# Layer normalisation in two rounds of four tiles instead of four rounds of two, and half of a preload moved to another queue

## The chip, the cores and the metric

The kernel runs on the 8 cores of one Trainium2 chip. Each core works on its own 1024 of the 8192 tokens, with all weights; the cores exchange nothing. The metric is the device time in microseconds (us) of the slowest core. A core has TensorE (PE, matmuls), VectorE (DVE), ScalarE (ACT), GpSimd (POOL) and SyncE (SP). SP, ACT and POOL issue transfers (DMA), each from a queue of its own; the profile names them q1 (SP), q10 (ACT) and q0 (POOL).

## The reference

```python
xn = _layernorm(x)                                   # over 4096 features
s  = einsum('bsk,nk->bsn', xn, weight * block_mask)  # 4096 x 4096, mask of 32x32 blocks
gt = einsum('th,ih->ti', xn, w_gate) * s_gate        # 11008 x 4096
u  = einsum('th,ih->ti', xn, w_up) * s_up
h  = silu(gt) * u
f  = einsum('ti,hi->th', h, w_down) * s_down         # 4096 x 11008
out = x + s * silu(f)
```

x is 4 x 2048 x 4096 in float32; the three big weights are int32 with values up to 127.

## The kernel before

The program has four blocks with a barrier after each: "prep", "attn", "ffnA", "down".

**prep** (from line 121) makes xnT, the normalised x of the core, transposed and in bf16. The 1024 tokens are 8 tiles j of 128 tokens by 4096 features. There are four buffers xs (float32) and four xn (bf16), used as xs[j % 4] and xn[j % 4]; tiles 0 to 3 are loaded at the start, in pairs from SP (0, 2) and ACT (1, 3), and SP then loads the small constants. For a tile:
- VectorE sums it (L172) after its load. ScalarE squares it with an accumulated sum (L196); the squared values themselves go to xn[j % 4] as scratch, so for j of 4 and more this waits until tile j-4 is normalised and transposed.
- `stats` (L148 to L168) makes mean, variance, reciprocal root and shift from these sums in small instructions on VectorE, with the root on ScalarE (L201) between.
- ScalarE normalises it into xn (L207). TensorE transposes it in 32 pieces (L239), into four PSUM tiles p_tr of eight pieces each, and VectorE copies each p_tr to xnT (`evac_tr`, L147). TensorE writes p_tr[b] for the next tile only after the copy of p_tr[b] of the last.

Before the change `stats` runs on two columns (tiles 2b and 2b+1), for b from 0 to 3. VectorE's order is: sum 2b, sum 2b+1, stats b, then the copies of tiles 2b-2 and 2b-1. ScalarE's order (`half`) is two squares, root, two normalisations. Tiles 4 and 6 are loaded by SP as soon as tiles 0 and 2 are normalised. Tiles 5 and 7 are loaded by ACT, between the halves, after tiles 1 and 3 are normalised (L217). VectorE begins with three copies of transposed scale vectors (L136), which come from constants that SP loads behind its two tiles of x.

The semaphore p1s counts ScalarE's instructions; `s_sq`, `s_sqrt_b` and `s_xn` give the count at which a square, a root or a normalisation is done.

**attn** (from line 306) loads the mask and the weight, multiplies them, and makes s. **ffnA** (from line 470) makes h for 86 tiles of 128 inner features and stores each to hTd in DRAM.

**down** (from line 581) multiplies h with w_down, in 8 groups g of 512 output features. The first 48 tiles of h are loaded once into hTr, by six transfers r of 2 MB (eight tiles each, L587). The other 38 come anew for each g, in pairs through four buffers hTl (L605). SP issues the six transfers of hTr first and then the pairs; after pair 2 it issues four tiles of x (L615). TensorE takes the tiles in the order P4SEQ, which mixes resident and streamed ones: 0, 48, 1, 49, 2, ... so the first pair hTl is wanted for the second of 86 steps of a group. ScalarE has nothing to do in down before the first group of matmuls is complete.

Of the kernel before, what the change touches and what calls it, by code (L numbers as in the profile page):

```python
# [13 lines left out]
AX = mybir.AxisListType  # L14
# [22 lines left out]
def build_nc():  # L37
# [20 lines left out]
    with ExitStack() as top:  # L58
# [25 lines left out]
        with ExitStack() as s123:  # L84
# [3 lines left out]
            if True:  # L88
                with ExitStack() as s01:
# [23 lines left out]

                    t_vtr = lambda k: k + 1
                    t_trb = lambda j, b: 3 + 4 * j + b + 1
                    s_sq = lambda j: 5 * (j // 2) + (j % 2) + 1
                    s_sqrt_b = lambda b: 5 * b + 3
                    s_xn = lambda j: 5 * (j // 2) + 4 + (j % 2)
                    V = {}

                    with nc.Block("prep") as blk:
                        @blk.vector
                        def _(ve):
                            vc = 0
                            def inc(ins):
                                nonlocal vc
                                ins.then_inc(p1v, 1)
                                vc += 1
                                return vc
                            inc(ve.memset(eps_col[:, :], EPS))  # L130
                            inc(ve.memset(invd_col[:, :], 1.0 / D))
                            inc(ve.memset(ninvd_col[:, :], -1.0 / D))
                            for k, dst in enumerate([(sg_cols, NIT), (su_cols, NIT),
                                                     (sd_cols, 32)]):
                                ve.wait_ge(p1t, t_vtr(k))
                                V[f"vecev{k}"] = inc(ve.tensor_copy(  # L136
                                    dst[0][:, 0:dst[1]], p_vec[k % 2][:, 0:dst[1]]))
                            def evac_tr(jj):
                                for b in range(4):
                                    ve.wait_ge(p1t, t_trb(jj, b))  # L140
                                    dst = xnT[:, :].rearrange(
                                        "p (kc t) -> p kc t", t=T)[
                                        :, b * 8:(b + 1) * 8,
                                        jj * 128:(jj + 1) * 128]
                                    src = p_tr[b][:, :].rearrange(
                                        "p (c t) -> p c t", t=128)
                                    V[f"trev{jj}_{b}"] = inc(ve.tensor_copy(dst, src))  # L147
                            def stats(b, sl, sqrt_lm):  # L148
                                n_mean = inc(ve.tensor_scalar(
                                    st_mean[:, sl], st_sum[:, sl],  # L150
                                    ninvd_col[:, 0:1], None, ALU.mult))
                                inc(ve.tensor_scalar(st_msq[:, sl], st_ssq[:, sl],
                                                     invd_col[:, 0:1], None, ALU.mult))
                                ve.wait_ge(p1v, n_mean)
                                n_m2 = inc(ve.tensor_tensor(
                                    st_m2[:, sl], st_mean[:, sl],
                                    st_mean[:, sl], ALU.mult))
                                ve.wait_ge(p1v, n_m2)
                                V[f"var_{b}"] = inc(ve.tensor_tensor(
                                    st_var[:, sl], st_msq[:, sl], st_m2[:, sl],  # L160
                                    ALU.subtract))
                                ve.wait_ge(p1s, sqrt_lm)
                                n_rst = inc(ve.reciprocal(st_rst[:, sl],
                                                          st_sqv[:, sl]))
                                ve.wait_ge(p1v, n_rst)
                                V[f"nmr_{b}"] = inc(ve.tensor_tensor(
                                    st_nmr[:, sl], st_mean[:, sl], st_rst[:, sl],
                                    ALU.mult))  # L168
                            for b in range(4):
                                for j in (2 * b, 2 * b + 1):  # L170
                                    ve.wait_ge(sm_x[j % 4], 16 * (j // 4 + 1))
                                    V[f"sum{j}"] = inc(ve.reduce_sum(  # L172
                                        st_sum[:, j:j + 1], xs[j % 4][:, :], AX.X))
                                ve.wait_ge(p1s, s_sq(2 * b + 1))
                                ve.wait_ge(p1v, V[f"sum{2 * b + 1}"])
                                stats(b, slice(2 * b, 2 * b + 2), s_sqrt_b(b))
                                if b >= 1:
                                    evac_tr(2 * b - 2)
                                    evac_tr(2 * b - 1)
                            evac_tr(6)  # L180
                            evac_tr(7)

                        @blk.scalar
                        def _(sc):
                            for i in (1, 3):
                                sc.dma_start(xs[i % 4][:, :],
                                             d_x[i * 128:(i + 1) * 128, :]
                                             ).then_inc(sm_x[i % 4], 16)

                            def half(js, var_lm, nmr_lm):  # L190
                                for j in js:
                                    sc.wait_ge(sm_x[j % 4], 16 * (j // 4 + 1))
                                    if j >= 4:
                                        sc.wait_ge(p1s, s_xn(j - 4))
                                        sc.wait_ge(p1t, t_trb(j - 4, 3))
                                    sc.activation(xn[j % 4][:, :], xs[j % 4][:, :],  # L196
                                                  AF.Square,
                                                  accum_out=st_ssq[:, j:j + 1]
                                                  ).then_inc(p1s, 1)
                                sc.wait_ge(p1v, V[var_lm])  # L200
                                sc.activation(st_sqv[:, js[0]:js[-1] + 1],  # L201
                                              st_var[:, js[0]:js[-1] + 1], AF.Sqrt,
                                              bias=eps_col[:, 0:1]).then_inc(p1s, 1)
                                sc.wait_ge(p1v, V[nmr_lm])
                                for j in js:
                                    sc.wait_ge(p1s, s_sq(j))
                                    sc.activation(xn[j % 4][:, :], xs[j % 4][:, :],  # L207
                                                  AF.Identity,
                                                  bias=st_nmr[:, j:j + 1],
                                                  scale=st_rst[:, j:j + 1]  # L210
                                                  ).then_inc(p1s, 1)
                            for b in range(4):
                                half([2 * b, 2 * b + 1], f"var_{b}", f"nmr_{b}")
                                if b <= 1:
                                    i = 2 * b + 5
                                    sc.wait_ge(p1s, s_xn(i - 4))
                                    sc.dma_start(xs[i % 4][:, :],  # L217
                                                 d_x[i * 128:(i + 1) * 128, :]
                                                 ).then_inc(sm_x[i % 4], 16)

                        @blk.tensor
                        def _(te):
# [326 lines left out]
        with ExitStack() as s4:  # L549
# [31 lines left out]
            with nc.Block("down") as blk:  # L581
                @blk.sync
                def _(sy):
                    for r in range(6):
                        sy.wait_ge(sm_hT_st[0], 16 * (4 * r + 4))
                        sy.wait_ge(sm_hT_st[1], 16 * (4 * r + 4))
                        sy.dma_start(  # L587
                            hTr[:, r * 8192:(r + 1) * 8192].rearrange(
                                "q (i t) -> q i t", i=8),
                            d_hTd[8 * r:8 * r + 8, :, :].rearrange(  # L590
                                "i q t -> q i t")).then_inc(sm_hr[r], 16)
# [88 lines left out]

                @blk.scalar
                def _(sc):
                    for g in range(8):
                        sc.wait_ge(p4t, g * NIT + NIT)
                        for ht in range(4):
# [80 lines left out]
```

## Time and profile before

| | |
|---|---|
| median of 8 runs | 4368.04 us (4361.84 to 4985.66) |
| profiled execution | 4363.12 us |
| its span, slowest core (0) | 4361.3 us; the eight cores 4347.6 to 4361.3 |
| mean granted TensorE clock, core 0 | 0.973 |
| TensorE matmuls busy | 4054.6 us, 93% |
| VectorE busy | 694.2 us, 16% |
| ScalarE busy | 210.9 us, 5% |
| moved by the DMA engines | 599.17 MB |

The profile is one execution, on its slowest core. Busy time is that of compute instructions; the issue of a transfer is shown on a queue (SPq, ACTq). The time from issue to landing is not busy time of any engine. The time of the whole execution lies 1.8 us above the span of the slowest core.

### The profile page before, as it was taken

The numbers are of one execution on the slowest core, as the hardware profiler recorded it, in microseconds if no ns is written. First come the engines' busy times: TensorE is split into PE (matmuls) and PEld (weight loads), VectorE is DVE, ScalarE is ACT, GpSimd is POOL, SyncE is SP. The second block draws the span as 40 slices with busy tenths as digits, with TensorE's granted clock in tenths as the row PEclk, the third lists the DMA queues.
The fourth block names the chain that finished last, engine by engine and source line by source line (L and its number), as shares of the span: only waits on it lengthen the run. The fifth ranks groups of instructions, "written<-read, shape, count | busy, mean of one in ns | idle before, by whom it ended". The sixth has DMA issues, their size and how long they took to land.

```text
span 4361.3 us, 43080 instructions; the slowest of 8 cores (4347.6 to 4361.3 us)
## 1 busy us (share of the span) xinstructions
PE 4054.6 (93%) x18669; PEld 1847.5 (42%) x19043; DVE 694.2 (16%) x584; ACT 210.9 (5%) x267; POOL 239.1 (5%) x384
## 2 busy tenths in 40 slices
PE   2199998999999999999999999999599999999998
PEld 1044443444444444444444444444244444444443
DVE  5577530000000000000000000000000000000000
ACT  5000000000000000000000000000000000000000
POOL 0000000000000000000000000000011111111110
PEclk8599999999999999999999999999799999999999
DMA  4899634444444444444444444443778888887886
GB/s 156 292 339 326 224 135 87 87 87 87 86 84 84 84 84 85 85 86 86 87 87 87 87 87 87 87 87 78 207 156 184 194 176 164 191 197 153 185 195 133
DMA packets 205543, 599.17 MB, mean 137 GB/s; under 512 B 13156, under 2 KB 101552, under 8 KB 174000
## 3 DMA queue, kind: packets, MB, share of 16 engines
q0 software_dynamic: 120256, 287.33, 37.9%
q1 hardware_dynamic: 62928, 252.96, 17.3%
q10 hardware_dynamic: 22176, 56.11, 3.6%
q8 instruction: 155, 2.54, 0.2%
q14 instruction: 28, 0.23, 0.0%
HBM read 810.79 MB, written 47.71 MB: 197 GB/s over the span
## 4 chain that ended last, share of the span: by engine, by line
PE 80%; DMA 2%; DVE 1%; SPq 1%; issue 1%; ACT 0%; DVEq 0%; POOL 0%; ACTq 0%
PE p_g L503 27%; PE p_u L503 27%; PE p_acc L677 26%; DMA hTl<-hTd 2%; SPq L587 1%; DVE tmpm L711 0%; DVE outs L714 0%; ACT gTs L689 0%; DMA wub<-hwu 0%; DMA hTd<-hTt 0%; DVE uss L538 0%; ACT L689 0%; DVE hTt L546 0%; SPq L615 0%; POOL wgb L476 0%
## 5 line engine op out<-in xcount | busy, mean ns | idle before, releaser
L503 PE MATMUL p_g<-xnT,wgb 128*128 128x512 bf16 x5394 | 1198.3, 380 | 25.1 <-DMA wub<-hwu 19.3
L503 PE MATMUL p_u<-xnT,wub 128*128 128x512 bf16 x5394 | 1195.7, 379 | 5.8
L503 PEld LDWEIGHTS p_g<-xnT,wgb 128*128 128x128 bf16 x5504 | 540.0, 98 | 670.1 <-issue 23.3
L503 PEld LDWEIGHTS p_u<-xnT,wub 128*128 128x128 bf16 x5504 | 537.7, 98 | 650.2
L677 PE MATMUL p_acc<-hTr,wdb 128*128 128x512 bf16 x3010 | 719.4, 380 | 38.5 <-ACT gTs L689 18.3
L677 PE MATMUL p_acc<-hTl,wdb 128*128 128x512 bf16 x2384 | 576.4, 382 | 41.8 <-DMA hTl<-hTd 39.1
L677 PEld LDWEIGHTS p_acc<-hTr,wdb 128*128 128x128 bf16 x3072 | 301.0, 98 | 410.0 <-issue 55.6
L538 DVE TENSOR_SCALAR uss<-p_u,su_cols 128x512 f32<-128x512 f32 x172 | 121.2, 746 | 2162.6 <-PE p_u L503 2162.6
L370 PE MATMUL p_sT<-xnT,wtm 128*128 128x512 bf16 x2004 | 444.8, 381 | 9.6 <-DVE wtm L421 6.7
L677 PEld LDWEIGHTS p_acc<-hTl,wdb 128*128 128x128 bf16 x2432 | 239.0, 98 | 331.4 <-issue 49.5
L370 PEld LDWEIGHTS p_sT<-xnT,wtm 128*128 128x128 bf16 x2048 | 199.0, 98 | 244.8 <-issue 10.0
L711 DVE TENSOR_TENSOR tmpm<-gTs,sTl 128x1024 f32<-128x1024 f32 x32 | 39.2, 1225 | 1208.9 <-ACT gTs L689 1206.4
L522 ACT ACTIVATE sil<-p_g,sg_cols 128x512 f32<-128x512 f32 x172 | 108.9, 684 | 2239.4 <-PE p_u L503 2239.4
L476 POOL DMA_DIRECT2D wgb<-hwg x86 | 45.8, 532 | 2916.4 <-PE p_u L503 2247.6
L637 POOL DMA_DIRECT2D wdb<-hwd x174 | 128.9, 741 | 1166.7 <-PE p_acc L677 1059.0
L421 DVE TENSOR_TENSOR wtm<-wts,p_me 128x4096 bf16<-128x4096 f32 x32 | 141.5, 4421 | 74.4 <-PE p_sT L370 57.3
L394 DVE TENSOR_REDUCE red<-mk 128x128 f32<-128x4096 int32 x32 | 141.3, 4414 | 49.8 <-DMA mk<-mask 49.7
L546 DVE TENSOR_TENSOR hTt<-sil,uss 128x1024 bf16<-128x1024 f32 x86 | 105.4, 1225 | 10.4 <-ACT sil L522 1.6
L339 PE MATMUL p_bm<-red,gm_sb 128*4 128x128 f32 x64 | 14.5, 315 | 86.9 <-DVE bmfeT L408 55.5
L689 ACT ACTIVATE gTs<-p_acc,sd_cols 128x512 f32<-128x512 f32 x64 | 37.9, 703 | 1041.2 <-PE p_acc L677 1041.2
L239 PE MATMUL p_tr<-idb_sb,xn 128*128 128x128 bf16 x256 | 22.0, 267 | 50.1 <-DVE xnT L147 33.5
L479 POOL DMA_DIRECT2D wub<-hwu x86 | 46.3, 538 | 2.8 <-issue 2.8
(43 smaller groups left out, 280.0 us busy)
## 6 DMA issues: line engine op xcount, KB each, us to landing
wgb<-hwg POOLq DMA_DIRECT2D x86, 1024.0 KB, 9.2
wub<-hwu POOLq DMA_DIRECT2D x86, 1024.0 KB, 13.9
wdb<-hwd POOLq DMA_DIRECT2D x168, 512.0 KB, 7.5
hTl<-hTd SPq DMA_DIRECT2D x152, 512.0 KB, 6.1
mk<-mask SPq DMA_DIRECT2D x32, 2048.0 KB, 12.9
wts<-hwt SPq DMA_DIRECT2D x32, 2048.0 KB, 11.2
hTd<-hTt ACTq DMA_DIRECT2D x86, 256.0 KB, 10.3
xTl<-xT SPq DMA_DIRECT2D x32, 512.0 KB, 11.6
```

What stands on the lines that cost most here:

```text
L370: ins = te.matmul(p_sT[par][th][:, :], A, xnT[:, kb * T + th * 512: kb * T + th * 512 + 512], start=(kb == 0), stop=(kb == 31))
L394: ve.tensor_reduce(red[k % 2][:, :], mk[k % 2][:, :].rearrange("p (s e) -> p s e", e=32), AX.X, ALU.add).then_inc(p2v, 1)
L421: ve.tensor_tensor(wtm[par][:, :].rearrange("p (a b c) -> p a b c", a=32, b=4), wts[par][:, :].rearrange("p (a b c) -> p a b c", a=32, b=4 ...
L476: gp.dma_start(wgb[it % 2][:, :].rearrange("p (b i) -> p b i", i=128), d_hwg[it]).then_inc(sm_wg[it % 2], 16)
L479: gp.dma_start(wub[it % 2][:, :].rearrange("p (b i) -> p b i", i=128), d_hwu[it]).then_inc(sm_wu[it % 2], 16)
L503: ins = te.matmul(p_x[th][:, :], A, xnT[:, blk_h * T + th * 512: blk_h * T + th * 512 + 512], start=(blk_h == 0), stop=(blk_h == 31))
L522: sc.activation(sil[par][:, th * 512:th * 512 + 512], p_g[par][th][:, :], AF.Silu, scale=sg_cols[:, it:it + 1]).then_inc(p3s, 1)
L538: ve.tensor_scalar(uss[par][:, th * 512:th * 512 + 512], p_u[par][th][:, :], su_cols[:, it:it + 1], None, ALU.mult).then_inc(p3v, 1)
L546: ve.tensor_tensor(hTt[par][:, :], sil[par][:, :], uss[par][:, :], ALU.mult).then_inc(p3v, 1)
L587: sy.dma_start(hTr[:, r * 8192:(r + 1) * 8192].rearrange("q (i t) -> q i t", i=8), d_hTd[8 * r:8 * r + 8, :, :].rearrange("i q t -> q i t" ...
L637: gp.dma_start(dst.rearrange("p (i hh) -> p i hh", i=nit), d_hwd[it0:it0 + nit, :, g, :, :].rearrange("i p a b -> p i (a b)")).then_inc(sm ...
L677: ins = te.matmul(p_acc[ht][th][:, :], A, B, start=(j == 0), stop=(j == NIT - 1))
```

## The change

In prep, `stats` runs twice, on four columns each (tiles 0 to 3, then 4 to 7). VectorE's order becomes: sums 0 to 3; stats a; sum 4; sum 5; copies of tile 0; sum 6; copies of tile 1; sum 7; copies of tile 2; stats b; copies of tiles 3 to 7. ScalarE's order becomes: four squares, root, four normalisations; then the loads of tiles 5 and 7; then the same for tiles 4 to 7. In down, the transfers r = 1, 3, 5 of hTr are issued from ScalarE's queue; SP keeps r = 0, 2, 4.

```diff
-                    s_sq = lambda j: 5 * (j // 2) + (j % 2) + 1
-                    s_sqrt_b = lambda b: 5 * b + 3
-                    s_xn = lambda j: 5 * (j // 2) + 4 + (j % 2)
+                    s_sq = lambda j: j + 1 if j < 4 else j + 6
+                    S_SQRT_A, S_SQRT_B = 5, 14
+                    s_xn = lambda j: j + 6 if j < 4 else j + 11
...
-                            for b in range(4):
-                                for j in (2 * b, 2 * b + 1):
-                                    ve.wait_ge(sm_x[j % 4], 16 * (j // 4 + 1))
-                                    V[f"sum{j}"] = inc(ve.reduce_sum(
-                                        st_sum[:, j:j + 1], xs[j % 4][:, :], AX.X))
-                                ve.wait_ge(p1s, s_sq(2 * b + 1))
-                                ve.wait_ge(p1v, V[f"sum{2 * b + 1}"])
-                                stats(b, slice(2 * b, 2 * b + 2), s_sqrt_b(b))
-                                if b >= 1:
-                                    evac_tr(2 * b - 2)
-                                    evac_tr(2 * b - 1)
-                            evac_tr(6)
-                            evac_tr(7)
+                            for j in range(4):
+                                ve.wait_ge(sm_x[j % 4], 16)
+                                V[f"sum{j}"] = inc(ve.reduce_sum(
+                                    st_sum[:, j:j + 1], xs[j % 4][:, :], AX.X))
+                            ve.wait_ge(p1s, s_sq(3))
+                            ve.wait_ge(p1v, V["sum3"])
+                            stats("a", slice(0, 4), S_SQRT_A)
+                            for j in range(4, 8):
+                                ve.wait_ge(sm_x[j % 4], 32)
+                                V[f"sum{j}"] = inc(ve.reduce_sum(
+                                    st_sum[:, j:j + 1], xs[j % 4][:, :], AX.X))
+                                if j >= 5:
+                                    evac_tr(j - 5)
+                            ve.wait_ge(p1s, s_sq(7))
+                            ve.wait_ge(p1v, V["sum7"])
+                            stats("b", slice(4, 8), S_SQRT_B)
+                            for j in range(3, 8):
+                                evac_tr(j)
...
-                            for b in range(4):
-                                half([2 * b, 2 * b + 1], f"var_{b}", f"nmr_{b}")
-                                if b <= 1:
-                                    i = 2 * b + 5
-                                    sc.wait_ge(p1s, s_xn(i - 4))
-                                    sc.dma_start(xs[i % 4][:, :],
-                                                 d_x[i * 128:(i + 1) * 128, :]
-                                                 ).then_inc(sm_x[i % 4], 16)
+                            half([0, 1, 2, 3], "var_a", "nmr_a")
+                            for i in (5, 7):
+                                sc.wait_ge(p1s, s_xn(i - 4))
+                                sc.dma_start(xs[i % 4][:, :],
+                                             d_x[i * 128:(i + 1) * 128, :]
+                                             ).then_inc(sm_x[i % 4], 16)
+                            half([4, 5, 6, 7], "var_b", "nmr_b")
...
-                    for r in range(6):
+                    for r in (0, 2, 4):
                         sy.wait_ge(sm_hT_st[0], 16 * (4 * r + 4))
                         sy.wait_ge(sm_hT_st[1], 16 * (4 * r + 4))
                         sy.dma_start(
...
                 @blk.scalar
                 def _(sc):
+                    for r in (1, 3, 5):
+                        sc.wait_ge(sm_hT_st[0], 16 * (4 * r + 4))
+                        sc.wait_ge(sm_hT_st[1], 16 * (4 * r + 4))
+                        sc.dma_start(
+                            hTr[:, r * 8192:(r + 1) * 8192].rearrange(
+                                "q (i t) -> q i t", i=8),
+                            d_hTd[8 * r:8 * r + 8, :, :].rearrange(
+                                "i q t -> q i t")).then_inc(sm_hr[r], 16)
```

## Rows read from the trace of the kernel before

**Rows 1.** The page, part 2: busy tenths in 40 equal slices.
```profile
PE   2199998999999999999999999999599999999998
DMA  4899634444444444444444444443778888887886
```

**Rows 2.** Timeline of ScalarE in prep: start us, us, queue or engine, line, operation.
```profile
1.06 0.90 ACTq L186 DMA_DIRECT2D xs<-x  x2
18.78 1.28 ACT L196 ACT_TABLE_LOAD   x1 [18.78 <-DMA xs<-x]
...
45.20 7.49 ACT L207 ACTIVATE xn<-xs,st_nmr,st_rst 128x4096 bf16<-128x4096 f32 x2 [0.68 <-DVE st_nmr L166]
52.77 0.33 ACTq L217 DMA_DIRECT2D xs<-x  x1
...
94.45 0.18 ACT L196 ACTIVATION_READ_ACCUMULATOR xn<-xs 128x1 f32 x1
...
96.64 7.49 ACT L207 ACTIVATE xn<-xs,st_nmr,st_rst 128x4096 bf16<-128x4096 f32 x2 [0.68 <-DVE st_nmr L166]
```

**Rows 3.** Timeline of VectorE in prep.
```profile
34.52 8.74 DVE L172 TENSOR_REDUCE st_sum<-xs 128x1 f32<-128x4096 f32 x2
43.38 0.23 DVE L149 TENSOR_SCALAR st_mean<-st_sum,ninvd_col 128x2 f32<-128x2 f32 x1
...
62.31 5.21 DVE L147 COPY xnT<-p_tr 128x1024 bf16<-128x1024 bf16 x8
...
94.81 0.23 DVE L149 TENSOR_SCALAR st_mean<-st_sum,ninvd_col 128x2 f32<-128x2 f32 x1 [1.26 <-ACT xn L196]
...
105.09 2.48 DVE L147 COPY xnT<-p_tr 128x1024 bf16<-128x1024 bf16 x4 [1.06 <-PE p_tr L239]
```

**Rows 4.** Timeline of SP's queue, prep and start of attn.
```profile
49.09 17.65 SPq L259 DMA_DIRECT2D xs<-x  x2
107.86 0.33 SPq L312 DMA_DIRECT2D e_sb<-e32f  x1
```

**Rows 5.** Timeline of TensorE in prep.
```profile
63.15 5.48 PE L239 MATMUL p_tr<-idb_sb,xn 128*128 128x128 bf16 x64 [10.43 <-DVE xnT L147]
```

**Rows 6.** Transfers issued at 48 to 53 and 70 to 75 us: KB, us to landing.
```profile
xs<-x SPq DMA_DIRECT2D x1, 2048.0 KB, 12.1
...
xs<-x ACTq DMA_DIRECT2D x1, 2048.0 KB, 12.3
```

**Rows 7.** Windows: us, busy by engine (x count), granted clock, DMA share, GB/s.
```profile
70.00:80.00 10.00, 0.00 (x0) 0.00 (x0) 7.36 (x9) 7.67 (x7) 0.00 (x0) 0.68 1.00 321
```

**Rows 8.** Timeline of VectorE, first work of attn.
```profile
128.69 4.42 DVE L394 TENSOR_REDUCE red<-mk 128x128 f32<-128x4096 int32 x1 [21.11 <-DMA mk<-mask]
```

**Rows 9.** Timeline of TensorE and SP's queue, ffnA to down.
```profile
3050.71 13.98 PE L503 MATMUL p_u<-xnT,wub 128*128 128x512 bf16 x63
3068.55 33.51 SPq L587 DMA_DIRECT2D hTr<-hTd  x6
3081.72 3.57 PE L677 MATMUL p_acc<-hTr,wdb 128*128 128x512 bf16 x8 [17.04 <-DMA hTr<-hTd]
3102.31 9.32 SPq L605 DMA_DIRECT2D hTl<-hTd  x3
3121.71 3.57 PE L677 MATMUL p_acc<-hTl,wdb 128*128 128x512 bf16 x8 [36.42 <-DMA hTl<-hTd]
```

**Rows 10.** Windows, the 60 us of the hand-over.
```profile
3065.00:3125.00 60.00, 6.86 (x16) 2.21 (x17) 2.50 (x3) 1.10 (x2) 1.48 (x2) 0.52 0.94 288
```

**Rows 11.** DMA totals of 3110 to 3122 us and of 3750 to 3765 us.
```profile
DMA packets 1908, 4.15 MB, mean 346 GB/s; under 512 B 84, under 2 KB 84, under 8 KB 1908
...
DMA packets 2352, 3.91 MB, mean 260 GB/s; under 512 B 128, under 2 KB 1229, under 8 KB 2351
```

**Rows 12.** DMA queues from 10 to 20 us: packets, MB, share of 16 engines.
```profile
q1 hardware_dynamic: 108, 1.51, 50.1%
q10 hardware_dynamic: 108, 1.51, 49.0%
```

More of the change, by code:

```diff
@@ L147, in evac_tr, with stats @@
                                     V[f"trev{jj}_{b}"] = inc(ve.tensor_copy(dst, src))
-                            def stats(b, sl, sqrt_lm):
+                            def stats(h, sl, sqrt_lm):
                                 n_mean = inc(ve.tensor_scalar(
@@ L158, in stats @@
                                 ve.wait_ge(p1v, n_m2)
-                                V[f"var_{b}"] = inc(ve.tensor_tensor(
+                                V[f"var_{h}"] = inc(ve.tensor_tensor(
                                     st_var[:, sl], st_msq[:, sl], st_m2[:, sl],
@@ L165, in stats @@
                                 ve.wait_ge(p1v, n_rst)
-                                V[f"nmr_{b}"] = inc(ve.tensor_tensor(
+                                V[f"nmr_{h}"] = inc(ve.tensor_tensor(
                                     st_nmr[:, sl], st_mean[:, sl], st_rst[:, sl],
                                     ALU.mult))
-                            for b in range(4):
-                                for j in (2 * b, 2 * b + 1):
-                                    ve.wait_ge(sm_x[j % 4], 16 * (j // 4 + 1))
-                                    V[f"sum{j}"] = inc(ve.reduce_sum(
-                                        st_sum[:, j:j + 1], xs[j % 4][:, :], AX.X))
-                                ve.wait_ge(p1s, s_sq(2 * b + 1))
-                                ve.wait_ge(p1v, V[f"sum{2 * b + 1}"])
-                                stats(b, slice(2 * b, 2 * b + 2), s_sqrt_b(b))
-                                if b >= 1:
-                                    evac_tr(2 * b - 2)
-                                    evac_tr(2 * b - 1)
-                            evac_tr(6)
-                            evac_tr(7)
+                            for j in range(4):
[16 more added lines that the diff above has]
+                                evac_tr(j)
                         @blk.scalar
```

## The prediction

> **What bounds the kernel now.** I read the page first. Its slices [rows 1] show TensorE full from the third slice on, but for one: the bulk of the span is matmuls that the diff does not touch. Two stretches are empty of matmuls and touched by the diff: the first slice (block "prep") and part of the 29th, around 3068 us, where "ffnA" hands over to "down". So I opened the timeline of each engine in these two stretches.
>
> In prep nothing is bound by one engine; it is a relay. ScalarE waits for the first tile of x until 18.78 us and then squares two tiles [rows 2]. VectorE starts to sum only at 34.52 us, because its first work waits for a small constant that lands late [rows 3]. Then for each pair of tiles: two sums (8.74 us), seven small instructions, two normalisations on ScalarE (7.49 us), transposes on TensorE, eight copies of p_tr on VectorE (5.21 us). The transposes follow the copies, since a bank of p_tr is written again only when it is copied [rows 5]. The last copy ends at 105.09 + 2.48 = 107.57 us [rows 3], and SP issues the first transfer of the next block at 107.86 us [rows 4]: a barrier, with no mask or weight loaded ahead. What prep loses, the rest loses too; the first mask is reduced at 128.69 us [rows 8], and that wait is for a load issued after the barrier.
>
> At the other stretch TensorE ends ffnA at 3050.71 + 13.98 = 3064.69 us, does eight matmuls at 3081.72 us when hTr group 0 is there, and then stands until 3121.71 us for the first pair hTl, which SP issued at 3102.31 us behind six transfers of hTr [rows 9]. Queue order put it there, but the limit is the transfers: the 16 DMA engines are busy for 0.94 of the 60 us, at 288 GB/s [rows 10]. Ahead of and with the first pair lie 6 x 2.10 + 0.52 = 13.1 MB.
>
> **Prep, part by part.** The change makes two statistics rounds of four, of four tiles each. Two rounds of small instructions go: in the round at 43.38 us there are 45.20 - 43.38 = 1.82 us from its first small instruction to the first normalisation [rows 2, 3]. They widen from 2 to 4 columns, which I cost at nothing: the bound is one 2-column instruction more, 0.23 us, a round [rows 3].
>
> First half. VectorE sums tiles 0 to 3 at 4.37 us each from 34.52: to 52.0. ScalarE's four squares are hidden under that: at two queues' 1.51 MB in 10 us each [rows 12] the four tiles' 8.4 MB are there by about 31 us, and two squares of 3.6 us (the tail of one is in [rows 2]) behind that end near 38. Statistics from 52.1; first normalisation at 52.1 + 1.82 = 53.9 (before: 45.20). Four of them at 3.70 us, the last 3.79: to 68.8.
>
> Now the loads. Tile j+4 can be loaded when tile j is normalised. Tile 4: SP issued it 3.89 us after the first normalisation began (49.09 - 45.20 [rows 2, 4]), now at 57.8, before 49.09. Tile 6: at 53.9 + 7.4 + 3.9 = 65.2, before about 66.4. But tiles 5 and 7 stand in ScalarE's own stream behind all four normalisations: tile 5 goes at 68.9 instead of 52.77 [rows 2], 16 us late; tile 7 at 69.3, before 70.09. A transfer of a tile with little beside it lands 12.1 to 12.3 us after issue [rows 6]. Tile 5 shares the engines with tile 6: the two in one stretch are 4.19 MB, at 321 GB/s [rows 7] 13.1 us from tile 6's first packet (65.2 + 3.7 = 68.9) to 82.0, and 1.9 us from last packet to landing (12.1 less 3.7 and less 2.10 MB at 321 GB/s). So tile 5 lands at 83.9. Bounds: 68.9 + 12.1 = 81.0, and 68.9 + 17.7 = 86.6, the 17.7 us of the first tile with four in flight (1.06 to 18.78 [rows 2]).
>
> Behind tile 5 everything is in one line, by the order written on VectorE: sum 5, copies of tile 0, sum 6, copies of tile 1, sum 7, copies of tile 2. ScalarE's square 7 writes xn3 and must wait for the transposes of tile 3, and these for the copies of tile 2. So, from the landing of tile 5: three sums 3 x 4.37 = 13.1; three times four copies 3 x 2.6 = 7.8; transposes after the last copy 1.1 (63.15 + 5.48 against 62.31 + 5.21 [rows 3, 5]); square 7 with its read 3.8, hand-over 0.2 (94.45 + 0.18 to 94.81); statistics 1.8; four normalisations 14.9; from the last normalisation to the last copy 107.57 - (96.64 + 7.49) = 3.4 [rows 2, 3]. Sum 46.2. Copies 3 to 6 are hidden under the four normalisations. If the transposes of tile 3 run slower than these (the granted clock is 0.68 in a stretch near by [rows 7]) I allow up to 0.6 us on top, of the 2.7 us that 32 of them take.
>
> Prep ends at 83.9 + 46.2 = 130.1 instead of 107.57: **+22.5 us**, bounds +19.6 and +25.8. Even if tile 5 had been there when VectorE was free (tile 4 lands at 57.8 + 12.1 = 69.9), four sums and three sets of copies from 69.9 end at 95.2, and with the same tail of 25.2 prep ends at 120.4: +12.8. So the order on VectorE alone costs that, and the late tile the other 9.7.
>
> **Down, part by part.** Three of the six transfers of hTr go to ScalarE's queue; SP is left with 3 x 2.10 + 0.52 = 6.8 MB up to the first pair, ScalarE gets 6.3 MB. Nothing waits behind ScalarE's three issues, its next work there being the first activation after a whole group of matmuls. When two queues had work in prep they were served alike, 1.51 MB and 1.51 MB in 10 us [rows 12]. Served alike, SP reaches the end of its 6.8 MB when ScalarE's 6.3 MB are through as well: 13.1 MB, as before. Group 0 lands later (it took 13 us, now up to a third share, some 22 us), but is covered: it is wanted for 3.6 us of matmuls ahead of 3121.7. The other groups are wanted later than the first pair. Cost **0**. Bounds by rate: 53 us of transfers at the 346 GB/s of the stretch in which only large packets moved instead of 288 would be -8.9 us, at the 260 GB/s of a stretch with several queues +5.7 [rows 11]. I take 0, since the engines are as busy with one queue as they can be [rows 10].
>
> The Trainium skill (DMA: Bandwidth & Descriptors, Issuing engines are not separate DMA queues) says that transfers from either engine run on the same 16 DMA engines and interleave, and that only the issuing time is saved; by that the down edit is worth 0. The trace agrees as far as it goes: share 0.94 with one queue [rows 10], equal halves with two [rows 12]. Read the other way, with a queue as a separate path, the 13.1 MB would take half of their 45 us and the sum would be about 23 us less.
>
> **Sum.** 4363.12 (the profiled execution) + 22.5 + 0 = 4385.6 us, said as 4386. That execution is 4.9 us under the median of the runs shown (4368.04); five of the eight lie between 4361.84 and 4368.06, so the same sum from the median would be 4391. I stay with the profiled one.
>
> **Rivals.**
> 1. The line on VectorE is shorter than I think because tile 5 is no later than the rest: +12.8, 4376 us. For it: nothing but that I composed the landing. Against: no tile landed under 11.8 us in any row I saw, and this needs 5.
> 2. SP's queue is served more than ScalarE's at the hand-over. This ends on the other side. Place: the first pair behind SP's three groups. With share s over one half, the pair lands after 6.8/s MB. At two thirds that is 10.2 MB, 10 us less: 4376. At all of it, 6.3 MB less at 288 GB/s, 21.8 us: 4364, no change. It decides from s = 0.75, where 13.9 us come back and the change is under 8.7 us. For it: the six issues of hTr take SP 33.5 us [rows 9], so a queue has limited room and two may be filled unevenly. Against: the equal halves [rows 12].
> 3. Prep does what fewer rounds promise: loads and copies hide, and ScalarE is the limit. From 69.6: four squares 14.5, hand-over 0.2, statistics 1.8, normalisations 14.9, tail 3.4: 104.4, or -3.2, 4360 us, no measurable change. Against: the waits above, which are in the code.
> 4. Rival 3 and the higher rate of the hand-over together: -12, 4351 us. The only way to a gain.
>
> **Chances.** 0.2% is 8.7 us, about what a measurement of this kernel can tell from no change. Forecast 0.83 (slower); rival 1 0.06 (slower); rival 2 between one half and 0.75 0.03 (slower), above 0.03 (same); rival 3 0.03 (same); rival 4 0.02 (faster). So slower 0.92, same 0.06, faster 0.02. Range: the lowest is tile 5 landing early and the better rate, 4363.1 + 19.6 - 8.9 = 4374; the highest 4363.1 + 25.8 + 5.7 = 4395, and 2 us more because the runs shown reach 4.9 us above the profiled one. I give 4374 to 4397, which takes in rival 1 and the mild form of rival 2.
>
> **What would show it.** In the timeline of the changed kernel: first normalisation at 53.9; ScalarE's issues of x at 68.9; VectorE standing from the end of sum 4 (74) to 84 for tile 5; square 7 near 106; four normalisations from 112; the first transfer of the next block at 130.4, not 107.9. In down: two queues with equal bytes, group 0 landing after some 20 us, matmuls on hTl beginning as long after the end of ffnA as before (57 us). The prediction is wrong if the next block starts before 120, or if the 57 us shrink by over 10.

## The result and the profile after

The changed kernel takes 1.0042 times the time of the one before, 95% interval 1.003 to 1.0054: some 18 us slower (13 to 24). Its profiled execution took 4383.99 us (span 4382.4) against 4363.12 us (4361.3). The plain median over all twelve of its runs, 4571 us, can't be set against the 4368 us of before: in eight of them one die or both showed a lower granted clock, as in some runs of the kernel before, and the ratio leaves such runs out on both sides.

The page, its slices. They answer to [rows 1]: the loss is in the first two slices, the hand-over in the 29th looks the same.

```profile
PE   1199998999999999999999999999599999999998
...
DMA  4699643444444444444444444443778888887885
```

The slowest core is now core 5, so rows of core 5 follow; before, it ended prep 0.55 us later than core 0 (first transfer of attn at 108.41 us instead of 107.86). Timeline of VectorE in prep, after (answers to [rows 3], [rows 8]; the sum of a tile starts when the tile is there, if VectorE is free):

```profile
35.02 17.39 DVE L171 TENSOR_REDUCE st_sum<-xs 128x1 f32<-128x4096 f32 x4
52.52 0.23 DVE L149 TENSOR_SCALAR st_mean<-st_sum,ninvd_col 128x4 f32<-128x4 f32 x1
...
70.99 4.42 DVE L178 TENSOR_REDUCE st_sum<-xs 128x1 f32<-128x4096 f32 x1 [16.77 <-DMA xs<-x]
80.40 4.42 DVE L178 TENSOR_REDUCE st_sum<-xs 128x1 f32<-128x4096 f32 x1 [4.99 <-DMA xs<-x]
84.74 2.48 DVE L147 COPY xnT<-p_tr 128x1024 bf16<-128x1024 bf16 x4
87.13 4.41 DVE L178 TENSOR_REDUCE st_sum<-xs 128x1 f32<-128x4096 f32 x1
91.46 2.47 DVE L147 COPY xnT<-p_tr 128x1024 bf16<-128x1024 bf16 x4
93.85 4.41 DVE L178 TENSOR_REDUCE st_sum<-xs 128x1 f32<-128x4096 f32 x1
98.17 2.47 DVE L147 COPY xnT<-p_tr 128x1024 bf16<-128x1024 bf16 x4
106.55 0.23 DVE L149 TENSOR_SCALAR st_mean<-st_sum,ninvd_col 128x4 f32<-128x4 f32 x1 [5.90 <-ACT xn L201]
...
124.24 2.48 DVE L147 COPY xnT<-p_tr 128x1024 bf16<-128x1024 bf16 x4 [1.21 <-PE p_tr L243]
147.00 4.42 DVE L398 TENSOR_REDUCE red<-mk 128x128 f32<-128x4096 int32 x1 [20.28 <-DMA mk<-mask]
```

VectorE stands 16.77 us for tile 4 and 4.99 us for tile 5. From 80.40 us on it has no gap until copy 2 is done at 100.64, then it waits 5.90 us for square 7. The first mask is reduced at 147.00 us instead of 128.69. Timeline of ScalarE, same stretch (answers to [rows 2]):

```profile
54.37 11.18 ACT L212 ACTIVATE xn<-xs,st_nmr,st_rst 128x4096 bf16<-128x4096 f32 x3 [0.70 <-DVE st_nmr L166]
61.94 0.33 ACTq L220 DMA_DIRECT2D xs<-x  x1
65.46 3.78 ACT L212 ACTIVATE xn<-xs,st_nmr,st_rst 128x4096 bf16<-128x4096 f32 x1
69.32 0.33 ACTq L220 DMA_DIRECT2D xs<-x  x1
71.09 3.62 ACT L201 ACTIVATE xn<-xs 128x4096 bf16<-128x4096 f32 x1 [1.84 <-DMA xs<-x]
74.61 0.19 ACT L201 ACTIVATION_READ_ACCUMULATOR xn<-xs 128x1 f32 x1
89.24 3.62 ACT L201 ACTIVATE xn<-xs 128x4096 bf16<-128x4096 f32 x1 [14.44 <-PE p_tr L243]
...
95.95 3.62 ACT L201 ACTIVATE xn<-xs 128x4096 bf16<-128x4096 f32 x1 [3.01 <-PE p_tr L243]
...
102.67 3.62 ACT L201 ACTIVATE xn<-xs 128x4096 bf16<-128x4096 f32 x1 [3.00 <-PE p_tr L243]
...
108.40 14.88 ACT L212 ACTIVATE xn<-xs,st_nmr,st_rst 128x4096 bf16<-128x4096 f32 x4 [0.70 <-DVE st_nmr L166]
```

Squares 5, 6 and 7 each wait for transposes (14.44, 3.01 and 3.00 us), and these for the copies above. The two views are to be read as one zigzag: sum, copies, transposes, square. The last transposes of this zigzag, those of tile 3 at 99.00 us, and others of a whole tile at 119.84, in the timeline of TensorE (answers to [rows 5]):

```profile
99.00 3.57 PE L243 MATMUL p_tr<-idb_sb,xn 128*128 128x128 bf16 x32 [3.14 <-DVE xnT L147]
119.84 1.95 PE L243 MATMUL p_tr<-idb_sb,xn 128*128 128x128 bf16 x32 [0.75 <-ACT xn L212]
```

The 32 transposes of a tile take 3.57 us in the first row and 1.95 us in the second. Square 7 starts 2.03 us after the end of the copies of tile 2 (102.67 - 100.64). Timeline of SP's queue (answers to [rows 4]):

```profile
58.26 7.72 SPq L263 DMA_DIRECT2D xs<-x  x2
127.01 0.33 SPq L316 DMA_DIRECT2D e_sb<-e32f  x1
```

The next block starts at 127.01 us instead of 108.41: +18.6 us. Over the eight cores its start lies at 122.5 to 127.0 instead of 106.9 to 108.7, on average at 124.5 instead of 107.9. The cores differ: on cores 1, 2, 4 and 6 the sum of tile 5 starts at 75.3 to 76.6 us and not at 78.4 to 80.4 as on the others, VectorE then stands 0.6 to 1.2 us for tile 6 too, and the next block starts at 122.5 to 124.1. The queues from 65 to 70 us, while tile 4 (SP) and tile 5 (ACT) are in flight:

```profile
q10 hardware_dynamic: 50, 0.82, 54.9%
q1 hardware_dynamic: 61, 0.75, 45.8%
```

Timeline of TensorE and SP's queue at the hand-over (answers to [rows 9]):

```profile
3068.39 13.98 PE L507 MATMUL p_u<-xnT,wub 128*128 128x512 bf16 x64
3102.26 26.12 SPq L609 DMA_DIRECT2D hTl<-hTd  x3
3107.68 3.57 PE L681 MATMUL p_acc<-hTr,wdb 128*128 128x512 bf16 x8 [25.32 <-DMA hTr<-hTd]
3140.60 3.57 PE L681 MATMUL p_acc<-hTl,wdb 128*128 128x512 bf16 x8 [29.35 <-DMA hTl<-hTd]
```

Group 0 is later (25.32 us of wait, before 17.04), the first pair comes 3140.60 - 3082.37 = 58.2 us after the end of ffnA; before it was 57.0 on core 0. Over the eight cores this stretch lasted 55.6 to 59.9 us before and 54.0 to 59.9 after, on average 57.4 and 57.0. SP issues the first pair much earlier, 3102.26 - 3082.37 = 19.9 us after the end of ffnA instead of 3102.31 - 3064.69 = 37.6; it lands no earlier for that. The windows of the same 60 us (answers to [rows 10]) and the queues of 3095 to 3105 us:

```profile
3085.00:3145.00 60.00, 7.97 (x19) 2.69 (x20) 0.28 (x1) 0.00 (x0) 1.49 (x2) 0.53 0.97 294
```

```profile
q1 hardware_dynamic: 508, 1.03, 35.8%
q0 software_dynamic: 509, 0.50, 34.9%
q10 hardware_dynamic: 507, 1.04, 33.1%
```

About the same rate (294 GB/s, before 288), now in three queues that are served packet for packet alike: 508, 509 and 507. From 3110 to 3130 us SP's and ScalarE's queue are served alike as well (731 packets each, then 771 and 768).

### The profile page after: what moved, and what is told of

Its sections match the earlier page's. It is cut to its first block and busy times, and to the rows that moved or that the text cites. A ratio compares the mean times of both kernels' runs of the same rounds, so it can differ in the third digit from the quotient of the medians.

```text
span 4382.4 us, 43424 instructions; the slowest of 8 cores (4360.6 to 4382.4 us)
## 1 busy us (share of the span) xinstructions
PE 4084.1 (93%) x19043; PEld 1851.3 (42%) x19043; DVE 692.6 (16%) x572; ACT 210.5 (5%) x265; POOL 238.7 (5%) x384
## 5 line engine op out<-in xcount | busy, mean ns | idle before, releaser
L681 PE MATMUL p_acc<-hTl,wdb 128*128 128x512 bf16 x2432 | 585.2, 384 | 29.3 <-DMA hTl<-hTd 29.3
L243 PEld LDWEIGHTS p_tr<-idb_sb,xn 128*128 128x128 bf16 x256 | 23.1, 132 | 67.6 <-issue 67.6
```

Of the source, the lines that this page charges most:

```text
L243: ins = te.transpose(p_tr[b][:, c * 128:(c + 1) * 128], xn[j % 4][:, kc * 128:(kc + 1) * 128], idb_sb[:, :])
L681: ins = te.matmul(p_acc[ht][th][:, :], A, B, start=(j == 0), stop=(j == NIT - 1))
```

## The experiments

All are compared with the kernel before, on the same chip; ratios with 95% intervals. "Start of attn" is the issue of that block's first transfer, on average over the eight cores: 107.9 us before, 124.5 in the changed kernel.

**The two halves of the change.** e1 has the change's prep and the down block of before:

```diff
-                    for r in (0, 2, 4):
+                    for r in range(6):
...
-                    for r in (1, 3, 5):
-                        sc.wait_ge(sm_hT_st[0], 16 * (4 * r + 4))
```

> The prep half of the change alone, down as before. My theory (all of the loss is in prep, the hand-over is worth 0): the next block's first transfer is issued at 122 to 127 us on the cores, as in the changed kernel, and the time is 1.0035 to 1.0045 of before (+15 to +20 us). Rival (the moved transfers of hTr cost or give back 5 us or more): this kernel differs from the full change by that much.

Measured: 1.0046 (1.0033 to 1.0059), attn starts at 124.4. All of the loss is there without the moved transfers. e2 is the reverse, the prep of before with the change's down block.

> The other half alone: hTr groups 1, 3, 5 from ScalarE's queue, prep as before. My theory: ratio 0.999 to 1.001, from the end of ffnA to the first matmul on hTl 57 to 60 us as before, group 0 some 25 us after the end of ffnA instead of 17. Rival (two queues move more, or SP's is served more): the stretch is 5 us or more shorter. Rival (the third queue slows the transfers): 5 us or more longer.

It gave a single time to compare, 4370.39 us against 4364.41 to 4368.13 of before, and so no interval. The same kernel was run again:

> e2_down_only once more, for an interval: ratio 0.999 to 1.001 if the moved transfers are worth nothing; 1.001 or more if the third queue costs; below 0.999 if it pays.

Measured: 1.0006 (0.9996 to 1.0016). Timeline of TensorE on its slowest core, at the hand-over:

```profile
3049.42 13.98 PE L503 MATMUL p_u<-xnT,wub 128*128 128x512 bf16 x64
3088.63 3.57 PE L677 MATMUL p_acc<-hTr,wdb 128*128 128x512 bf16 x8 [25.24 <-DMA hTr<-hTd]
3121.68 3.57 PE L677 MATMUL p_acc<-hTl,wdb 128*128 128x512 bf16 x8 [29.48 <-DMA hTl<-hTd]
```

58.3 us from the end of ffnA to the first pair: group 0 late, the pair not. The interval holds no change; a gain above 0.04% and a cost above 0.16% (7 us) are outside it.

**The order on VectorE.** e3 is e1 with the copies of tiles 0 to 3 moved ahead of sums 4 to 7:

```diff
                             stats("a", slice(0, 4), S_SQRT_A)
+                            for j in range(4):
+                                evac_tr(j)
                             for j in range(4, 8):
...
-                                if j >= 5:
-                                    evac_tr(j - 5)
...
-                            for j in range(3, 8):
+                            for j in range(4, 8):
                                 evac_tr(j)
```

> As e1_prep_only, but VectorE copies tiles 0 to 3 out of p_tr right after the first statistics, ahead of sums 4 to 7. My theory (the line sum, copies, sum, copies, sum, copies, square 7 is the larger part of the loss): sums 5 to 7 follow the landings, the second statistics start at 93 to 95 us instead of 106.5, the next block's first transfer goes at about 114 us, +6 against before, 12 to 13 less than e1. Rival (the late tile 5 is the loss and the order costs nothing): within 3 us of e1.

Measured: 1.0014 (1.0 to 1.0027), attn starts at 113.1, 11.3 us before e1. Timeline of VectorE on its slowest core:

```profile
66.37 2.48 DVE L147 COPY xnT<-p_tr 128x1024 bf16<-128x1024 bf16 x4 [1.20 <-PE p_tr L243]
70.06 2.48 DVE L147 COPY xnT<-p_tr 128x1024 bf16<-128x1024 bf16 x4 [1.21 <-PE p_tr L243]
72.47 4.41 DVE L180 TENSOR_REDUCE st_sum<-xs 128x1 f32<-128x4096 f32 x1
79.76 13.07 DVE L180 TENSOR_REDUCE st_sum<-xs 128x1 f32<-128x4096 f32 x3 [2.88 <-DMA xs<-x]
92.94 0.23 DVE L149 TENSOR_SCALAR st_mean<-st_sum,ninvd_col 128x4 f32<-128x4 f32 x1
```

Tile 5 is as late as in the changed kernel (79.76), but the second statistics start at 92.94 instead of 106.55: the copies now lie in time in which VectorE stood. Two thirds of the loss, 11.3 of the 16.5 us of e1, were order.

**The late tile.** e4 is e1, order kept, with tiles 4 to 7 all on SP's queue:

```diff
-                            for i in (5, 7):
-                                sc.wait_ge(p1s, s_xn(i - 4))
-                                sc.dma_start(xs[i % 4][:, :],
...
-                            for i in (4, 6):
+                            for i in (4, 5, 6, 7):
```

> As e1_prep_only, order on VectorE kept, but tiles 4 to 7 are all loaded from SP's queue, one behind the other, so tile 5 doesn't share the engines with tile 6. If tile 5's landing is what the line waits for: tile 5 lands at about 77 us instead of 80.4 and the next block starts 3 us earlier than in e1. If VectorE's own work sets the line: no more than 1 us. If one queue is slower than two: later than in e1.

Measured: 1.0034 (1.0021 to 1.0046); the six times behind the ratio, 4378.3 to 4382.4, all lie under the six of e1, 4383.2 to 4387.8. Attn starts at 120.6, 3.8 us before e1. Timeline of VectorE on its slowest core:

```profile
67.73 4.42 DVE L178 TENSOR_REDUCE st_sum<-xs 128x1 f32<-128x4096 f32 x1 [13.97 <-DMA xs<-x]
74.64 4.42 DVE L178 TENSOR_REDUCE st_sum<-xs 128x1 f32<-128x4096 f32 x1 [2.49 <-DMA xs<-x]
```

On this core tile 5 is there at 74.64 us; in e1 it was at 79.81. Over the eight cores its sum starts at 73.9 instead of 77.6, 3.8 us earlier where 3 were expected, and attn starts 3.8 us earlier: everything behind moves with it. Tile 4 gains too (67.73 here, 70.44 in e1), since tile 5 no longer shares the engines with it.

**What starts the relay.** e5 is the kernel before, with VectorE's three copies of scale vectors (L136) behind sums 2 and 3:

```diff
+                            def vecev():
+                                for k, dst in enumerate([(sg_cols, NIT), (su_cols, NIT),
...
                                         st_sum[:, j:j + 1], xs[j % 4][:, :], AX.X))
+                                if b == 1:
+                                    vecev()
                                 ve.wait_ge(p1s, s_sq(2 * b + 1))
```

> The kernel before, with only VectorE's three copies of the transposed scale vectors moved from its first place to behind sums 2 and 3. Before, sum 0 started at 34.5 us, 16 us after its tile had landed. Theory (prep is one relay, and what starts its first statistics moves its end): sum 0 at 19 to 20 us, first statistics at 28 instead of 43.4, next block's first transfer at 92 to 94 us instead of 107.9, ratio 0.996 to 0.997. Rival (later tiles' landings or ScalarE limit prep, so an early start is lost): under 5 us come through.

Measured: 0.9961 (0.9946 to 0.9975), attn starts at 91.5. Timeline of VectorE, its slowest core:

```profile
18.72 8.74 DVE L173 TENSOR_REDUCE st_sum<-xs 128x1 f32<-128x4096 f32 x2 [17.47 <-DMA xs<-x]
27.59 0.23 DVE L150 TENSOR_SCALAR st_mean<-st_sum,ninvd_col 128x2 f32<-128x2 f32 x1
...
39.96 0.24 DVE L137 COPY sg_cols<-p_vec 128x86 f32<-128x86 f32 x1
...
89.31 2.48 DVE L148 COPY xnT<-p_tr 128x1024 bf16<-128x1024 bf16 x4 [0.77 <-PE p_tr L242]
```

The first statistics move from 43.38 to 27.59 us, the last copy from 105.09 to 89.31: 15.8 us at both ends. Here prep has no slack behind its first statistics, and the change moved just those the other way, from 43.38 to 52.52.

**Rounds of four with all of this mended.** e6 has the edits of e3, e4 and e5 (its `vecev()` stands behind sum 3) on the change's prep.

> Rounds of four with everything mended that the other runs found: copies of tiles 0 to 3 ahead of sums 4 to 7, tiles 4 to 7 all loaded from SP, the three copies of scale vectors behind sum 3; down as before. Theory (the batch itself costs: the first statistics wait for four tiles, the last at 35 to 40 us, and all later landings hang on them): first statistics at about 40 us instead of 52.5 in e3 and 28 in e5, next block at 101 to 103 us, ratio 0.998 to 0.999, so better than before but some 9 us behind e5, which keeps rounds of two. Rival (fewer rounds pay once nothing else is in the way): as good as e5 or better, ratio 0.996 or less.

Measured: 0.9982 (0.9971 to 0.9993), attn starts at 99.3. Timeline of VectorE, its slowest core:

```profile
30.62 8.75 DVE L172 TENSOR_REDUCE st_sum<-xs 128x1 f32<-128x4096 f32 x2 [3.12 <-DMA xs<-x]
...
40.24 0.23 DVE L150 TENSOR_SCALAR st_mean<-st_sum,ninvd_col 128x4 f32<-128x4 f32 x1
```

Even so the first statistics wait for tiles 2 and 3 (30.62) and start at 40.24, where rounds of two have theirs at 27.59. e5's edit is in e6, and by itself it gave more (0.9961) than e6 gives; the batch stays 8 us behind e5 in the start of attn and 0.2% in time.

**The hand-over.** e7 is the kernel before with another order on SP's queue: the first pairs go ahead of the later groups, and the four tiles of x go behind group 5 instead of pair 2. The waits for stored tiles of h become one for all 48 ahead of group 0; with it group 0 is there 17.1 us after the end of ffnA on average over the cores, before 16.5. Prep and all bytes stay as before.

```diff
-                    for r in range(6):
-                        sy.wait_ge(sm_hT_st[0], 16 * (4 * r + 4))
...
+                    hr(0)
...
+                            if g == 0 and p in (2, 3, 5, 7, 9):
+                                hr({2: 1, 3: 2, 5: 3, 7: 4, 9: 5}[p])
-                            if p == 2:
+                            if p == (10 if g == 0 else 2):
```

> The kernel before, with the queue order in down changed: SP issues hTr group 0, pairs 0 to 2, group 1, pair 3, group 2, pairs 4 and 5, group 3, pairs 6 and 7, group 4, pairs 8 and 9, group 5, then the tiles of x. Same bytes, all from SP. Theory (the first pair's place in the queue costs the wait, and the groups aren't wanted in the first 20 us): first matmul on hTl 20 to 25 us after the end of ffnA instead of 57, ratio 0.992 to 0.995, some of it given back as short waits in the first group. Rival (the limit is that 13.1 MB have to be moved, whatever the order): the waits come back at groups 1 and 2 and less than 10 us are gained.

Measured: 0.9941 (0.9923 to 0.9959), 26 us (18 to 34). e8 has e5's edit and e7's:

> e5 and e7 together. Both gains are in different blocks with a barrier between them, so they should add: the ratio is 1 less both losses within 0.001. Rival (the later blocks run into each other's transfers on the other core of a pair): less than the sum by 5 us or more.

Measured: 0.9907 (0.9892 to 0.9923), 4322.39 to 4325.67 us: the two gains add (0.0039 + 0.0059 = 0.0098 against 0.0093). It is faster than both kernels. Timeline of TensorE in down on its slowest core, the rows of the first group of matmuls with a wait for a transfer:

```profile
3065.62 3.57 PE L683 MATMUL p_acc<-hTr,wdb 128*128 128x512 bf16 x8 [17.67 <-DMA hTr<-hTd]
...
3104.40 3.49 PE L683 MATMUL p_acc<-hTl,wdb 128*128 128x512 bf16 x8 [3.41 <-DMA hTl<-hTd]
...
3139.39 1.89 PE L683 MATMUL p_acc<-hTl,wdb 128*128 128x512 bf16 x8 [2.06 <-DMA hTl<-hTd]
...
3156.20 1.89 PE L683 MATMUL p_acc<-hTl,wdb 128*128 128x512 bf16 x8 [1.10 <-DMA hTl<-hTd]
...
3166.74 3.17 PE L683 MATMUL p_acc<-hTl,wdb 128*128 128x512 bf16 x8 [3.48 <-DMA hTl<-hTd]
```

The 36 us of standing are gone; four short waits of 1 to 3.5 us come in the first group instead, 10.1 us in all, since the later groups still have to be moved meanwhile. On average over the cores the first pair comes 20.4 us after the end of ffnA in e7 and 20.2 in e8, instead of 57.4. Of these 37 us some 11 were given back, for the ratio of e7 is worth 26.

## Why the prediction held, and where it was off

It was right in sign and place, and the size lies in the given range: 4385.6 us were forecast, the profiled execution took 4383.99, and the ratio says +18 us where +22.5 were forecast. That it came so near is in part luck, for several terms were off and partly cancel.

- **A relay with a barrier behind it.** Held: attn starts 18.6 us later on core 5 and 16.6 later on average over the cores, the execution is 20.9 us longer (4383.99 against 4363.12), the ratio says 18. e1 carries the whole loss. The forecast was made for one core; on the four cores with an early tile 5 it is 7 to 9 us off at that landing, and why they get the tile earlier stays open.
- **First half.** Held: statistics at 52.52 (forecast 52.1), first normalisation at 54.37 (53.9), tile 4 issued at 58.26 (57.8).
- **Issue of tile 5: wrong.** I had it at 68.9, "behind all four normalisations". It went at 61.94, the moment normalisation 1 ended, with normalisations 2 and 3 still to be done: the row lies inside the one of three that runs from 54.37 to 65.55. Of the two loads only tile 7's, which truly depends on normalisation 3, went at 69.32.
- **Landing of tile 5: the term that was mis-sized.** I gave it 15.0 us from issue, shared with tile 6 alone. It took 18.5 (61.94 to 80.40), because tile 4 was still in flight too: from 65 to 70 us SP's queue, with tile 4, moved 0.75 MB and ScalarE's, with tile 5, 0.82. The two errors partly cancel: 80.4 instead of 83.9. That this landing sets the line is shown by e4. Also, the 3.7 us that I put from issue to first packet stand in no row; in the changed kernel tile 4, issued at 58.26, has its first packets at 60.6, after 2.4 us. The sum doesn't feel it, since what is less ahead of the first packet is more behind the last.
- **From the landing of tile 5 to the end of prep.** Forecast 46.2 us, measured 126.72 - 80.40 = 46.3. So near by luck: three sums with their copies took 20.2 us (80.40 to 100.64) where I had 20.9, and from the last copy to square 7 it took 2.0 where I had 1.1, for the transposes of tile 3 took 3.57 us. The allowance of 0.6 for that was too small.
- **Order and late tile.** I gave the order on VectorE 12.8 us and the late tile the other 9.7. With the order mended and the tile as late as ever, e3 takes away 11.3 of the 16.5 us and leaves 5.2; the tile 3.8 us earlier takes away 3.8 (e4). So the order is the larger part, as forecast, and the late tile was given too much.
- **Statistics on four columns at no cost.** Held: 0.23 us for the first instruction with 2 columns and with 4.
- **Down at 0.** Held. Both queues are served alike, group 0 comes 21.5 us after its issue (3086.20 to 3107.68; forecast some 22), 8 us later than before, and is covered. e2b bounds the worth; rival 2 (SP served more) falls by the packet counts, and because the first pair, issued 17.7 us earlier, landed no earlier.
- **Rivals 1, 3 and 4.** Tile 5 was awaited (4.99 us), which ends rival 1; and even with everything mended, rounds of four aren't as fast as rounds of two (e6 against e5), which ends rival 3, and 4 with it.
- **What bounds the hand-over: half wrong.** I wrote that queue order put the first pair last, "but the limit is the transfers". The engines are busy, but the bytes ahead of the pair aren't wanted then; e7 gets 26 us from order alone. The forecast for this change didn't hang on it.

What the batch costs by itself, after the mending, is shown only in sum (e6 against e5); how it splits between the later start and the later loads was not tried.

## What to carry to other kernels

Batching small instructions pays only if nothing large waits for the batch: here 1.8 us a round were saved on paper, and four tiles' loads, squares and copies were hung on the last tile of each batch. When an order is written by hand, draw the line from one landing to the end through every engine, with its buffer waits; that sum came out right, with parts off by 0.7 and 0.9 us, while the landing itself was off by 3.5 on the slowest core and by more on others. And busy DMA engines don't say that their order is right: moving half of a preload to another queue was worth nothing that could be measured (1.0006), putting the bytes that are wanted first at the head of the same queue was worth 0.6%.
